# Regrouping the expert-choice mixture of a two-layer decoder: power first, gate chain inside the expert loop, the second product's two sides in turn, and a scatter in two halves

## The reference

```python
rms = jnp.sqrt(jnp.mean(xf * xf, axis=-1, keepdims=True) + EPS)
xn = xf / rms * norm_weight
logits = xn @ router_weight.T + router_bias
probs = jax.nn.softmax(logits, axis=-1)
_, idx = jax.lax.top_k(logits.T, top_k)          # 16 x 64
xe = xn[idx]
h = jnp.einsum('ecd,efd->ecf', xe, fc1_weight) + fc1_bias[:, None, :]
h = jax.nn.gelu(h, approximate=False)
y = jnp.einsum('ecf,edf->ecd', h, fc2_weight) + fc2_bias[:, None, :]
gates = jnp.take_along_axis(probs.T, idx, axis=1)
output = zeros.at[idx].add(y * gates); gate_sums = zeros.at[idx].add(gates)
output = jnp.where(assigned, output / gate_sums, output)
x = _layernorm(x + output)
```

## Time and profile before

| what | value |
|---|---|
| median of 3 runs (lowest, highest) | 690.74 us (686.35, 692.92) |
| the profiled execution: its own time | 685.71 us |
| its span in the trace | 684.0 us |
| share of the span busy: PE, DVE, ACT, POOL | 76%, 55%, 32%, 22% |
| mean granted TensorE clock, of full speed | 0.888 |

### The profile page before, as it was taken

One profiled execution on the slowest core, in us unless ns is written; L12 is line 12 of the kernel. 1 busy time (PEld: TensorE's weight loads), 2 busy tenths in 40 slices (PEclk: granted clock), 3 DMA queues, 4 the chain that ended last, 5 costly groups with the idle time before them and its releaser, 6 DMA issues. The chain is left out here.

```text
span 684.0 us, 10410 instructions
## 1 busy us (share of the span) xinstructions
PE 522.5 (76%) x3892; PEld 263.0 (38%) x3940; DVE 372.9 (55%) x835; ACT 218.6 (32%) x441; POOL 150.3 (22%) x190
## 2 busy tenths in 40 slices
PE   4579999988888989330679966394888787589994
PEld 2433444544343434110248762244432343233331
DVE  2336554785675763339945433735386762444464
ACT  1112455436555466210011102330215575111211
POOL 8063315342222300250000001220543000300000
PEclk9579999999999999855689998679598999889998
DMA  9431103011111100070000003000231000000000
GB/s 313 179 93 47 49 11 86 18 50 49 43 38 48 48 2 3 15 264 0 1 1 1 1 1 138 1 0 0 55 85 47 3 3 1 0 1 0 0 17 16
DMA packets 19811, 29.57 MB, mean 43 GB/s; under 512 B 2609, under 2 KB 18481, under 8 KB 19249
## 3 DMA queue, kind: packets, MB, share of 16 engines
q1 hardware_dynamic: 19760, 28.90, 13.5%
HBM read 15.52 MB, written 0.52 MB: 23 GB/s over the span
## 5 line engine op out<-in xcount | busy, mean ns | idle before, releaser
L877 DVE TENSOR_REDUCE nmax<-bank 128x2 f32<-128x512 f32 (+2 forms) x240 | 142.9, 625 | 101.3 <-PE bank L684 41.2
L787 ACT ACTIVATE arena<-bank 128x512 f32<-128x512 f32 (+2 forms) x256 | 128.6, 524 | 123.7 <-PE bank L688 40.5
L684 PE MATMUL bank<-arena 62*128 62x256 bf16 (+2 forms) x512 | 87.5, 260 | 14.9 <-DVE nmax L877 5.6
L688 PE MATMUL bank<-arena 64*128 64x256 bf16 (+2 forms) x512 | 87.1, 259 | 4.7 <-ACT arena L787 4.1
L447 PE MATMUL bank<-causal_qk,identb 128*128 128x512 bf16 x221 | 74.9, 428 | 20.4 <-PEq L917 8.9
L727 PE MATMUL bank<-arena 128*32 128x256 f32 (+4 forms) x1088 | 60.8, 344 | 2.3 <-ACT arena L787 2.1
L684 PEld LDWEIGHTS bank<-arena 62*128 62x128 bf16 x512 | 31.7, 95 | 72.6 <-issue 38.8
L447 PEld LDWEIGHTS bank<-causal_qk,identb 128*128 128x128 bf16 x266 | 25.9, 107 | 52.4 <-issue 29.0
L553 POOL TENSOR_TENSOR arena<-qk,arena 128x512 bf16<-128x512 f32 x16 | 18.6, 1160 | 111.5 <-ACT arena L749 111.2
L688 PEld LDWEIGHTS bank<-arena 64*128 64x128 bf16 x512 | 32.5, 95 | 18.3 <-ACT arena L787 11.3
L575 POOL TENSOR_SCALAR veps<-mv 128x2 f32<-128x2 f32 x12 | 2.6, 219 | 160.0 <-DVE mv L849 160.0
(11 more groups left out here) (276 smaller groups left out, 864.8 us busy)
## 6 DMA issues: line engine op xcount, KB each, us to landing
arena<-arena SPq DMA_DIRECT2D x96, 128.0 KB, 2.4
fcw<-in_fc1T SPq DMA_DIRECT2D x1, 4096.0 KB, 18.3
arena<-in_fc2T SPq DMA_DIRECT2D x1, 4096.0 KB, 14.1
fcw<-in_last SPq DMA_DIRECT2D x1, 2304.0 KB, 8.7
w<-in_w SPq DMA_DIRECT2D x1, 1216.0 KB, 6.1
rows<-in_rows SPq DMA_DIRECT2D x1, 704.0 KB
xT<-in_xT SPq DMA_DIRECT2D x1, 512.0 KB, 3.6
x<-in_x SPq DMA_DIRECT2D x1, 512.0 KB, 7.6
```

The costliest lines, as they stand in the source:

```text
L684: mins = t.matmul(mout[:, i, :], stack_rows(m, nm, h0 + i, 0, MAX_ROWS)[:, qt * P:(qt + 1) * P], stack_rows(m, nm, h0 + i, 1, MAX_ROWS)[:, ...
L688: sins = t.matmul(sout[i], stack_rows(m, nh, h, 1, SCORE_ROWS)[:, i * P:(i + 1) * P], stack_rows(m, nh, h, 0, SCORE_ROWS)[:, spans[i][0]:s ...
L787: s.activation(m.prob[h % 8][:, 0:w], ST[c % NST][:, 0:w], ACT.Exp).then_inc(exps, 1)
L877: v.tensor_reduce(m.nmax[n % 2][:, qt, h0:h0 + nh], MX[c % NMX][:, 0:nh * (k1 - k0)].rearrange("p (h k) -> p h k", h=nh), AX.X, ALU.max, n ...
```

## The change

Only `expert_choice` changes; the lines of code after it move down by some 67.

- GpSimd's power stands ahead of all constants but two `iota`; `ones` and `esel` come after the three terms. Slots are numbered from 1, which drops the -1 and the cast after the scan; `taken`, `count` and `posb` are bf16, and the transpose of the numbers is in bf16.
- TensorE transposes the tokens before the norm weight is applied; the weight comes in as a per-partition scale of ScalarE's copy (`norm_col`, made by one transpose and a one-column copy at the start). VectorE's multiply by it runs beside that.
- VectorE ranks before it looks at the transposed logits. TensorE does 18 `keep_warm` matmuls after the seventh MAX8.
- The gather's two banks are signalled apart. The gate chain is cut into `softmax`, `assigned`, `gate_terms` and `slot_gates`, placed in the expert loop; the 64 gate matmuls follow pair 3. Broadcasts run one pair ahead instead of two. The 12 `keep_warm` ahead of the loop become 1, the 12 behind it go.
- In the second product the two sides take turns. The outputs are weighed, split and scattered in two groups of four pairs, and the norm runs by halves, with two powers.

```diff
 # GpSimd
+            pool.wait_ge(ms_ready, 1)
+            g.tensor_tensor(m.rstd[:, :], m.veps[:, :], m.eps[:, 0:1].broadcast_to([P, TILES]), ALU.pow).then_inc(rs_ready, 1)
...
+            pool.wait_ge(xnT_mm, 8)
             pool.wait_ge(xn_ready, 1)
...
 # TensorE
-            pe.wait_ge(xn_ready, 1)
+            t.transpose(B[7][:, 0:P], row(m, "moe_norm"), m.ident[:, :]).then_inc(col_mm, 1)
+            pe.wait_ge(xs_ready, 1)
...
+            pe.wait_ge(rounds, CAP // 8 - 1)
+            keep_warm(nc, m, B[7], F_ROUTE)
             pe.wait_ge(pos_ready, 1)
...
-                for half in range(2):
-                    for f in range(FT):
+                for f in range(FT):
+                    for half in range(2):
                         ins = t.matmul(B[4 + r // 4][64 * half:64 * half + 64, (r % 4) * D:(r % 4 + 1) * D],
...
-                if r + 2 < PAIRS:
-                    broadcast(r + 2)
+                if r + 1 < PAIRS:
+                    broadcast(r + 1)
                 if r >= 1:
                     second(r - 1)
+                if r == 3:
+                    slot_gates()
             second(PAIRS - 1)
-
-            keep_warm(nc, m, B[7], 3 * WARM // 2)
...
+            scatter(0)
+            scatter(1)
 # ScalarE
-                s.copy(xnT[:, 512 * c:512 * c + 512], B[c][:, :]).then_inc(xnT_in, 1)
+                s.activation(xnT[:, 512 * c:512 * c + 512], B[c][:, :], ACT.Copy, scale=norm_col[:, :]).then_inc(xnT_in, 1)
 # VectorE
+            slots_of(0)
+            softmax()
+            for r in range(PAIRS):
+                if r + 1 < PAIRS:
+                    slots_of(r + 1)
+                bias_in(r)
+                if r == 0:
+                    assigned()
+                if r == 1:
+                    gate_terms()
+                if r == 4:
+                    for k in range(4):
+                        slot_gates(k)
+                if r == 5:
+                    for k in range(4, PAIRS):
+                        slot_gates(k)
+                    weighed(0)
+                if r == 6:
+                    y_terms(0)
+            weighed(1)
+            y_terms(1)
```

More of the change, by code:

```diff
@@ L420 @@
 F_EXPERT = 1
+F_ROUTE = 18
 WARM = 8
@@ L1073, in second, with slot_gates, scatter @@
                 ins.then_inc(y_mm, 1)
-            keep_warm(nc, m, B[7], 3 * WARM // 2)
+            def slot_gates():
+                pe.wait_ge(gl_ready, 1)
+                for r in range(PAIRS):
+                    for i in range(TILES):
+                        ins = t.matmul(B[6][:, r * 3 * E0:(r + 1) * 3 * E0], onehot[:, i, r * P:(r + 1) * P],
+                                       gl[:, i, :, :].rearrange("p l e -> p (l e)"), start=(i == 0), stop=(i == TILES - 1))
+                ins.then_inc(gs_mm, 1)
+            def scatter(c):
+                pe.wait_ge(ygl_ready, c + 1)
+                for i in range(TILES):
+                    for r in range(4 * c, 4 * c + 4):
+                        for l in range(3):
+                            ins = t.matmul(B[6 + i // 4][:, (i % 4) * D:(i % 4 + 1) * D], onehotT[:, r, i * P:(i + 1) * P],
+                                           ygl[:, l, r, :], start=(i % 4 == 0 and r == 0 and l == 0), stop=(r == PAIRS - 1 and l == 2),
+                                           skip_group_check=True)
+                    if c == 1:
+                        ins.then_inc(out_mm, 1)
             for r in range(PAIRS):
@@ L1133, in _ @@
             dve.wait_ge(rs_ready, 1)
-            link(v.tensor_tensor(xn, x2[:, :, :], m.rstd[:, :].unsqueeze(2).broadcast_to([P, TILES, D]), ALU.mult))
-            v.tensor_tensor(xn, xn, row(m, "moe_norm").unsqueeze(1).broadcast_to([P, TILES, D]), ALU.mult).then_inc(xn_ready, 1)
+            v.tensor_tensor(m.x[1][:, :, :], x2[:, :, :], m.rstd[:, :].unsqueeze(2).broadcast_to([P, TILES, D]), ALU.mult).then_inc(xs_ready, 1)
+            dve.wait_ge(xs_ready, 1)
+            v.tensor_tensor(xn, m.x[1][:, :, :], row(m, "moe_norm").unsqueeze(1).broadcast_to([P, TILES, D]), ALU.mult).then_inc(xn_ready, 1)
             dve.wait_ge(lg_in, 2)
+            for i in range(CAP // 8):
+                src = logits if i == 0 else work
+                v.max(top8[:, :], src[:, :]).then_inc(rounds, 1)
+                dve.wait_ge(rounds, i + 1)
+                link(v.match_replace(out=work[:, :], in_to_replace=top8[:, :], in_values=src[:, :], imm_value=TAKEN))
+            dve.wait_ge(const, 3)
+            link(v.tensor_scalar(taken, work[:, :], TAKEN, None, ALU.is_equal))
+            link(v.tensor_tensor_scan(count, ones[:, :], taken, 0.0, ALU.mult, ALU.add))
+            v.tensor_tensor(posb[:, :], count, taken, ALU.mult).then_inc(pos_ready, 1)
             dve.wait_ge(lgT_mm, 8)
@@ L1205, in _, with softmax @@
-            for c in range(2):
+            def softmax():
+                dve.wait_ge(ex_in, 1)
+                link(v.tensor_reduce(red[:, :], gate[:, :, :], AX.X, ALU.add))
+                link(v.reciprocal(inv[:, :], red[:, :]))
+                link(v.tensor_tensor(gate[:, :, :], gate[:, :, :], inv[:, :].unsqueeze(2).broadcast_to([P, TILES, E0]), ALU.mult))
+                link(v.tensor_scalar(pick[:, :, :], posT[:, :, :], 1.0, None, ALU.is_ge))
+                link(v.tensor_tensor(gate[:, :, :], gate[:, :, :], pick[:, :, :], ALU.mult))
@@ L1206, in _, with slot_gates, weighed @@
+            def slot_gates(r):
+                dve.wait_ge(gs_mm, 1)
+                for half in range(2):
+                    e = 2 * r + half
+                    part = B[6][64 * half:64 * half + 64, r * 3 * E0:(r + 1) * 3 * E0].rearrange("p (l e) -> p l e", l=3)
+                    ins = v.tensor_reduce(gslot[64 * half:64 * half + 64, r:r + 1], part[:, :, e], AX.X, ALU.add)
+                ins.then_inc(gs_in, 1)
+            def weighed(c):
                 dve.wait_ge(y_mm, 4 * c + 4)
+                dve.wait_ge(gs_in, 4 * c + 4)
@@ new lines, in _ @@
+            dve.wait_ge(const, 2)
+            dve.wait_ge(w_in, 80)
+            slots_of(0)
+            softmax()
+            for r in range(PAIRS):
+                if r + 1 < PAIRS:
[14 more added lines that the diff above has]
+                    y_terms(0)
@@ L1219, in norm_tiles, with norm_out @@
+            def norm_out(c):
+                dve.wait_ge(rstd_ready, c + 1)
+                for i in range(4 * c, 4 * c + 4):
+                    link(v.tensor_scalar(x3[:, i, :], x2[:, i, :], m.mv[:, i, 0:1], m.rstd[:, i:i + 1], ALU.subtract, ALU.mult))
+            norm_half(0)
+            norm_half(1)
+            norm_out(0)
+            norm_out(1)
 def norm_tiles(nc, m, dve, link, x, part, y, part_ready, var_ready, rstd_ready):
```

168 lines of the change are left out of this document (73 added, 95 removed).

## The result

| | before | after |
|---|---|---|
| median (lowest, highest) | 690.75 us of 4 runs (686.35, 692.92) | 664.09 us of 4 runs (658.35, 670.91) |
| ratio, 95% interval | | 0.961 [0.955, 0.966] |
| profiled execution, its span | 685.71, 684.0 | 662.31, 660.6 |
| the stage of the change: start, length | 287.09, 126.67 | 288.81, 100.38 |
| from its end to the span's end, code not touched | 270.24 | 271.41 |

A run over 1.5% above the lowest of its kernel is left out of the ratio: here the highest after, and further down three of the six of e11. The change makes the kernel 26.7 us faster by the medians; 666.8 was predicted. The stage got 26.3 us shorter. The span got only 23.4 shorter, because the stages around it, which run the same code, took 1.7 and 1.2 us more in this execution.

What follows compares the result with a forecast made beforehand. Waits between engines, not a busy engine, were taken to set the 126.7 us stage. Gains of 5.3 + 0.7 + 10.8 + 7.1 = 23.9 us off the 690.74 median gave 666.8 us, range 661 to 673.

Steps and rivals of the forecast that it cites:

- head: Stage start to first MAX8: earlier power 2.75, weight multiply off the path 1.25, softmax steps behind ranking 1.35; 5.3 us gained.
- ranking: First MAX8 to one-hots: dropping the -1 gains 0.7 us; the multiply ahead stays at its fp32 price.
- warm matmuls, gather: The 18 warm matmuls in the ranking hold nobody up and gain nothing; one-hots to gather's end stays 13.5 us.
- gather to first product: Between gather and first expert product: the first product starts 0.7 us after the gather instead of 11.5, 10.8 us gained.
- loop and tail: First product to stage end: 50.5 us instead of 57.6, 7.1 gained, 5.5 of it scatter beside vector work.
- rival of 1.9 us: At the gather: the warm matmuls hold the clock through it, 1.9 us more gained, 664.9 us; chance 0.17.
- sign of being wrong that I named: At the gather: the prediction is wrong if the gather stays at the low clock beyond its first eight matmuls.
- s: In the expert loop: time of one second product with sides in turn, taken as 1.0 us, ends 1.51 and 0.76.
- the walk: Expert loop and tail followed engine by engine from the first product at 0: loop ends at 33.55 us, tail at 50.5.
- rival of no alternation: In the second products: taking turns brings nothing, each stays 1.51 us, end 2.5 us later, 669.3 us; chance 0.14.
- rival of switches that serialise: In the second products: every switch of side serialises load and matmul, 6.56 us each, 709.5 us; chance 0.02.
- GpSimd in the way: In the first ranking rounds: GpSimd's terms hold them up by at most 5.8 us, 672.6 us; chance 0.07.

Runs made afterwards that it cites:

- e11: e10 with 11 warm matmuls at the start of the stage; stage 96.39 us, median of six runs 662.01 us, ratio to before 0.950.
- e5: Changed kernel with GpSimd's power back behind all its constants; stage 105.47 us against 100.38, profiled time 674.72 us.
- e6: Changed kernel with the whole gate chain back ahead of the expert loop; stage 103.23 us against 100.38, profiled time 673.33 us.
- e7: Changed kernel with 12 warm matmuls instead of 1 ahead of the first product; stage 105.30 us against 100.38, profiled time 664.78 us.
- e9: Changed kernel with the first scatter half waiting for the terms of both groups; stage 107.42 us against 100.38, profiled time 664.31 us.
- e1: Changed kernel with the second product's two sides one after the other again; stage 103.79 us against 100.38, profiled time 664.38 us.
- e3: Changed kernel without the 18 warm matmuls in the ranking; stage 101.38 us against 100.38, profiled time 665.07 us.
- e4: Changed kernel with 8 more warm matmuls between the transposes of the numbers and the gather; stage 99.67 us against 100.38, profiled time 657.73 us.
- e10: Changed kernel with the edits of e4 and e8 together; stage 98.45 us, median of six runs 659.17 us, ratio to before 0.954.
- e12: The changed kernel run again, unaltered; stage 99.84 us, median of six runs 664.05 us, ratio to before 0.961.
- e8: Changed kernel with the first half's terms moved behind the last bias; stage 97.30 us against 100.38, profiled time 660.64 us.
- e2: Kernel before with only the second product's two sides taking turns; stage 126.95 us against 126.67, profiled time 685.75 us.

## Why the prediction was right, step by step

| step of the prediction | predicted gain | measured | what differs |
|---|---|---|---|
| head | 5.3 | 5.6 | step 0.17 and power as said; logits depend on the clock |
| ranking | 0.7 | 1.9 | mis-sized |
| warm matmuls, gather | 0 | 0.3 | clock rose, fell just before the gather |
| gather to first product | 10.8 | 10.8 | |
| loop and tail | 7.1 | 7.7 | loop 33.47 (33.55 said), tail 16.47 (16.95 said) |
| stage | 23.9 | 26.3 | |

**Bounds.** That waits and not an engine set the stage's length held: four waits were put back or lengthened alone, and each showed at its place (e5 2.7, e6 4.8, e7 2.4, e9 4.1 and more).

**Head.** The order of GpSimd's list was worth the 2.75 of the sum, and e5 shows both parts of it, the power's place and the step at 0.70 beside constants. The other two terms no run put back; the traces have them at their size. The transposes start 5.81 us after the stage's start instead of 9.82, which is 2.76 and 1.25, and the first MAX8 stands 0.03 us behind the logits instead of 1.37. The 0.3 beyond the forecast lie in the logits. The scaled copy, costed at nothing, took 0.74 us a half where a plain one takes 0.6, so 0.15 to 0.3. Between executions the first MAX8 moved by 1.2 us with unchanged code (10.94 to 12.18) with the time that the logits took, 3.57 us in e1 and e5, 2.91 in the changed kernel and 2.35 in e6, depending on when the clock rose. The forecast named no such spread.

**Ranking.** This is the term that was off. The multiply of two packed bf16 inputs took 0.68 us for 1024 elements, not the 1.23 I carried over from fp32. The Trainium skill, VectorE: DVE Perf Modes, section Mode 2x_1P, has such work run at two elements a cycle; the trace agrees, with 1.23 / 0.68 = 1.8, and its total of 666.2 was the better one. I had weighed the page against the one-hots' 1.15, whose inputs are broadcast, and that was the wrong row to lean on. The other 0.7 of the difference are the transposes of the numbers in bf16: they took 0.35 us instead of 1.03, and from the last step on the numbers (324.50) to the first one-hot (325.27) it is 0.77 us instead of 1.45. It is not the clock, for in e3 they took 0.35 at the low clock, at which they ran before. I had taken them as unchanged.

**Warm matmuls.** The forecast of nothing and the rival of 1.9 us both occur: 0 to 0.3 in five executions, 1.7 in three. I put 0.17 on the rival; the runs say three in eight. By e3 the changed kernel's profile owed them at most 0.3, and with the last gap filled the gather was short in all three executions (e4, e10, e11). The sign of being wrong that I named, a gather at the low clock beyond its eighth matmul, was drawn too sharply: the kernel before left the low clock with its eighth, the changed kernel with its seventh, and e1 and e5, with the same code there, with their eleventh.

**Gather to first product.** The size was right. Of the 10.8 us, 5.0 are the warm matmuls, twelve at the low clock against one at the high: eleven of them cost 2.4 at the high clock (e7), and the other 2.6 are what the low clock added. The gate chain is 2.3 by e6. The remaining 3.5 no run put back. By the trace of before they lie in the second broadcast and the wait of 3.08 us ahead of it, which would make them the worth of broadcasting one pair ahead instead of two; that is argued and not shown. The prediction had listed these one-hots without a price. That the first product's clock "cannot have dropped" after a dense gather held here, at 1.00, but is no rule: see the last section.

**Loop.** s was taken as 1.0 and measured 1.03. The two waits, 0.4 and 1.85 in the walk, were 0.35 and 1.76. The walk stands at the high clock throughout; in e5 and e12, where the clock fell in the last wait, the same loop took 34.35. The rival of no alternation would have cost 2.5; e1, which is that rival, cost 2.4. The rival of switches that serialise fell: 32 records with a switch of side at each call of two records went through in 2.19 us (e8). The Trainium skill, TensorEngine Tiling (Array Packing), Key Properties, has no drain between tiles of one mode, and by that row there is none.

**Tail.** As walked, with 0.5 less behind the scatter: from its end to the first output step it is 2.56 us instead of the walk's 3.03, since residual and statistics of one half, with the statistics in a row, took less than I had allowed. e9 gives the price of the scatter's early start alone, 4.1 of the 5.5 that the prediction ascribes to scatter beside vector work; in e9 the first half's weighing and terms are still done inside the loop.

**GpSimd in the way** fell: rounds lasted 2.56 us each with GpSimd's terms beside them and without.

**The whole.** The span fell by 23.4, close to the 23.9 of the sum, but part of that is chance: the stage gained 2.4 more, and the code around it gave 2.9 back. The medians, 26.7 apart, are near the stage's gain, but with runs from 658.35 to 670.91 that nearness proves little. The median of 664.09 also lies closer to the 664.9 of the rival with a warm gather than to the forecast, and that is chance: in the changed kernel's profile the gather began at the low clock, and the difference is the mis-sized ranking.

## What to carry to other kernels

Where waits set a stage's length, walk each engine's list once with measured durations, the two engines that hand over above all. Here this gave a loop of 33.55 us where 33.47 were measured, and the last two waits to 0.1 us. Then look at what stands ahead of the last short instruction that another engine waits for; four terms moved behind one bias gave 1.1 us (e8). Judge a step of 1 to 3 us at its place in the trace and in several executions, for in one execution the clock can give or take as much somewhere else, as it did with the whole of e2's gain.

## What the runs showed of the hardware that was not expected

**The clock differed with the same instructions.** In e12 it fell near 475 us, in layer 1's attention, and stayed low for some 30 us while TensorE was recorded busy for 28.2 of 30 (475 to 505 us); the same code in e10 ran at the high clock. Busy time and granted clock of that stretch, first e12, then e10:

```profile
478.00:488.00 10.00, 10.00 (x30) 2.15 (x28) 6.03 (x11) 0.00 (x0) 5.81 (x7) 0.50 0.29 79
488.00:498.00 10.00, 10.00 (x38) 3.87 (x38) 5.27 (x11) 2.73 (x4) 0.00 (x0) 0.50 0.01 2
```

```profile
475.00:485.00 10.00, 9.43 (x49) 3.34 (x48) 8.75 (x18) 1.64 (x2) 5.49 (x7) 1.00 0.30 80
485.00:495.00 10.00, 7.30 (x84) 3.22 (x83) 7.55 (x13) 6.88 (x13) 5.41 (x7) 1.00 0.16 43
```

The first stretch of e12 has 30 matmuls, that of e10 49. The stretch behind the stage took 277.7 us in e12 and 267.3 in e10; e5, e6 and e11 show the same, with 277.6 to 277.7. Over whole runs the mean granted clock goes with the time: 0.904 in e12's two runs at 658 us, 0.882 and 0.887 in its two at 667; of before, 0.888 in the fastest run and 0.870 in the slowest. Whether it is this stretch also in the runs without a profile is not shown, and what starts it was not tried.

**Waits of equal length left the clock high or low.** A wait of 1.75 us ahead of the last second product left it high in four profiles; in two it fell in the wait and in one just behind it; 2.86 us ahead of the scatter left it high before, and 2.87 low in e2. In the changed kernel and e12 the code is the same.

**Small instructions of GpSimd and VectorE ended with the other engine's longer one.** GpSimd's two casts in the changed kernel's head ended at 294.66 and 295.87, and the two-input multiplies of VectorE that ran beside them at 294.57 and 295.83. In e5 a cast ended at 291.24 and the multiply at 291.15, and VectorE's eight-element step at 293.14, 0.04 after the memset of GpSimd beside it. The one-element cast took 1.15 us so, and 0.19 in e5 beside a reduction. It would fit that the two keep each other out of something they share, for the length of one instruction; that was not tried by itself. The rounds of the ranking, MAX8 and replace, showed nothing of it beside GpSimd's terms and memsets.
